# Loading the stacked queries and keys of an attention layer: six transfers from ScalarE's queue in place of nine from SyncE's

## The chip, the cores and the metric

The kernel runs on one core of one Trainium2 chip. The metric is device time in microseconds (us) of one execution. Lower is better. A core has five engines that run their own instruction streams and meet at semaphores: TensorE (PE in the rows, its weight loads are PEld), VectorE (DVE), ScalarE (ACT), GpSimd (POOL) and SyncE (SP), which here only issues transfers. Transfers run on 16 DMA engines that all queues share. A queue is written SPq, ACTq or POOLq after the engine that issues on it.

## The reference, cut to what matters

Two transformer blocks over x of shape (8, 512, 128), both with modulated layer norms. The first block has a linear attention and a mixture of 8 experts of which two are chosen for each token. The second block has the softmax attention that the change touches, and a mixture with one expert for each token:

```python
def _L1_attn_ref(x, Wq, bq, Wk, bk, Wv, bv, gamma, beta):
    H = 8
    B, S, D = x.shape            # 8, 512, 128
    dk = D // H                  # 16
    ...
    q = (xn @ Wq + bq).reshape(B, S, H, dk).transpose(0, 2, 1, 3)
    k = (xn @ Wk + bk).reshape(B, S, H, dk).transpose(0, 2, 1, 3)
    v = (xn @ Wv + bv).reshape(B, S, H, D).transpose(0, 2, 1, 3)
    scores = jnp.einsum('bhsd,bhtd->bhst', q, k) / jnp.sqrt(jnp.asarray(dk, x.dtype))
    p = jax.nn.softmax(scores, axis=-1)
    att = jnp.einsum('bhst,bhtd->bhsd', p, v)
    out = att.reshape(S, B, D, H).sum(axis=-1).reshape(B, S, D)
```

## The kernel before, in words

Each engine has an order written out by hand in the table ORDERS: a list of work items `kind.i.j` that its loop runs through. An engine never takes a later item before an earlier one, so an item that waits holds up everything behind it on its engine. The batches are taken in 4 pairs in the first block and one by one, 0 to 7, in the softmax attention.

For one batch i of that attention the items are these. `cpq` (TensorE, ScalarE, VectorE) makes q and k of all heads and splits each number into three bf16 terms, the last two of them made by `cpt` on GpSimd. `cto` (SP, line 554) writes the terms, 2 x 3 x 128 x 512 bf16, to the DRAM tensor `split`. `cst` (SP, lines 563 and 565) reads them back in another layout: for q and for k a stack of 96 partitions, six blocks of the 16 numbers of a head, where a partition holds 8 heads x 512 tokens = 8 KB. Every pair of blocks of the two stacks is one product of terms, so that one matmul with 96 rows gives the scores to nearly full precision. q's stack takes its three transfers of 48, 32 and 16 partitions (line 563), k's takes six of 16 partitions (line 565). `s1` (TensorE, line 1539) multiplies the stacks to the scores; `mx` (VectorE, line 1199) takes their maxima; `mt` (TensorE line 1545, ScalarE line 881, VectorE line 1217) puts the maxima into 12 more partitions of the stack; `s2` (TensorE, line 1555) makes the scores again, transposed and less their maxima; `ex` (ScalarE, line 888) takes the exponentials; `pv` (line 1565) multiplies them with v. Sixteen tiles of four `s2` and four `ex` make up a group of 4 heads.

There are two buffers for the stacks, so `cst` of batch i waits for the terms in DRAM (t_out) and, from batch 2 on, for the last `s2` that reads the buffer (c_s2x). `cto` of batch i + 1 waits until the stacks of batch i have landed (s_in), since both use the one tensor `split`. `s1` of a batch waits for s_in too.

Around it, the experts of the first block are still running on TensorE until about 425 us: `bw` (SP, line 520) loads the 514 KB of weights of one tile, `bh` and `by` (TensorE, lines 1504 and 1512) use them, with ScalarE's gelu (line 847) between the two. Five weight buffers go round, so `bw` waits for the `by` five tiles back. `bxl` (SP, line 529) loads sorted tokens, `byo` (SP, line 539) stores results, and GpSimd's indirect transfers (lines 691, 702) scatter and gather. Towards the end the routing of the last mixture does the same on lines 578 (`rxl`), 587 (`rw`), 590 (`ryo`) and 723 (`rsc`), with `rxt` (line 1404) and `rdx` (line 1410) on TensorE.

Of the kernel before, what the change touches and what calls it, by code (L numbers as in the profile page):

```python
# [12 lines left out]
B, S, D = 8, 512, 128  # L13
# [9 lines left out]
H1, DH1 = 8, 16  # L23
# [36 lines left out]
def same_rows(n):  # L60
# [198 lines left out]
def build(nc, io, out):  # L259
    ctx = ExitStack()  # L260
    with ctx:
# [101 lines left out]
        at = ab.o  # L363
# [8 lines left out]
        ex = ab.base[:, at:at + TILES * (E - 1)].rearrange("p (t e) -> p t e", t=TILES)  # L372
# [26 lines left out]
        qst = [stk[:, k] for k in range(2)]  # L399
        kst = [stk[:, 2 + k] for k in range(2)]  # L400
# [19 lines left out]
        split = dram("split", [2, 3, P, S], bf16)  # L420
# [24 lines left out]
        t_out = sem("c_terms_out")  # L445
        s_in = [sem(f"c_stacks_in{k}") for k in range(2)]
# [47 lines left out]
        def _(eng):  # L494
# [27 lines left out]
            for kind, i, j in ORDER["SP"]:  # L522
# [231 lines left out]
        def _(a):  # L754
# [5 lines left out]
            for kind, i, j in ORDER["ACT"]:  # L760
# [73 lines left out]
                if kind == "bxt":  # L834
                    q, n = TG * i + j, P * len(tiles_of(j))
# [5 lines left out]
                if kind == "bh":  # L841
                    n = TILES * i + j
# [33 lines left out]
                if kind == "mt":  # L876
                    b, h = group(i)
# [12 lines left out]
                if kind == "pvo":  # L890
# [3 lines left out]
                    b, h = group(i)  # L894
# [5 lines left out]
                if kind == "rxt":  # L900
                    n = P * len(tiles_of(j))
# [441 lines left out]
        def _(pe):  # L1343
# [3 lines left out]
            rows = identb[:, :].unsqueeze(1).broadcast_to([P, 4, P])  # L1347
# [18 lines left out]
            for kind, i, j in ORDER["PE"]:  # L1366
# [9 lines left out]
                if kind == "pc":  # L1376
                    pe.wait_ge(ld["mod"], 32)
                    pe.wait_ge(s_cs, 1)
                    for l in range(2):
                        for j6 in range(6):  # L1380
                            at = 8 * (6 * l + j6)
                            last = nc.tensor.matmul(ps[:, at:at + 8], wmod[:, l, D * j6:D * j6 + D], cs[:, l, :], start=True, stop=True)
                    last.then_inc(s_mod_c, 1)
                if kind in ("pm", "pr"):
                    n, rows2, js = (2 * i + j, (2 * j, 2 * j + 1), ROWS[i]) if kind == "pm" else (4, (0, 1), (3, 4))
                    pe.wait_ge(s_wide, n + 1)
                    for r in rows2:
                        for k in range(len(js)):
                            at = 512 * (r % 2) + D * k
# [263 lines left out]
```

## Time and profile before

| | |
|---|---|
| three runs, us | 791.36, 793.49, 792.43 |
| median | 792.43 |
| span of the profiled execution, first to last instruction | 674.4 us |
| TensorE busy | 601.6 us (89%) |
| VectorE busy | 481.1 us (71%) |
| ScalarE busy | 391.4 us (58%) |
| GpSimd busy | 330.5 us (49%) |
| mean granted TensorE clock | 0.978 |

The profile gives the span of its one execution and not that execution's own device time. The median less the span is 792.43 - 674.4 = 118.0 us; it lies before the first and after the last instruction that the span counts. All points in time below are microseconds from the span's start. A timeline row gives start, length, engine, line, operation, destination <- source and how many instructions are merged in it; square brackets give idle time of the engine before the row and what ended it.

### The profile page before, as it was taken

To read this page: it belongs to the slowest core of one execution; us is meant where nothing else is said; L and a number is where in the kernel's file an instruction comes from. 1 tells how busy PE (TensorE), PEld (TensorE's weight loads), DVE (VectorE), ACT (ScalarE), POOL (GpSimd) and SP (SyncE) were. 2 spreads that over 40 slices of the span, in tenths; PEclk is the share of its full clock that TensorE was granted. 3 is DMA by queue.
4 is the path that set the end of the run, shared out by engine and by line. 5 is a ranking of instruction groups with operands and counts; after the bars stand their busy time and mean duration, and the time that the engine had idled before them with its cause. 6 is when DMAs were issued, how large, how long until landed. Compare 5 with 4: busy or idle time off the path is not lost. (4 is left out here: it accounts for less than half of the span.)

```text
span 674.4 us, 11980 instructions
## 1 busy us (share of the span) xinstructions
PE 601.6 (89%) x3825; PEld 379.6 (56%) x3825; DVE 481.1 (71%) x1275; ACT 391.4 (58%) x866; POOL 330.5 (49%) x363
## 2 busy tenths in 40 slices
PE   8978988999999899798989899898999898889974
PEld 5656557988888797674345688332343324523332
DVE  4478876761794439388869734898998873889897
ACT  3444045889666575448778666676756576455510
POOL 5203378065478764704872601557456464064523
PEclk9999999999999999899999989999989998999999
DMA  8200415677789887949396868117411739311021
GB/s 336 116 1 2 141 44 168 213 247 251 249 304 311 283 315 238 285 151 252 119 232 196 167 234 268 40 40 173 70 25 36 170 114 214 102 47 48 17 63 31
DMA packets 47421, 106.40 MB, mean 158 GB/s; under 512 B 7440, under 2 KB 22608, under 8 KB 45824
## 3 DMA queue, kind: packets, MB, share of 16 engines
q1 hardware_dynamic: 41808, 94.82, 47.3%
q0 software_dynamic: 5120, 10.50, 4.9%
q8 instruction: 31, 0.51, 0.3%
q10 hardware_dynamic: 432, 0.34, 0.2%
q14 instruction: 30, 0.25, 0.1%
HBM read 80.26 MB, written 25.17 MB: 156 GB/s over the span
## 5 line engine op out<-in xcount | busy, mean ns | idle before, releaser
L1199 DVE TENSOR_REDUCE mxs<-PS 128x2 f32<-128x1024 f32 x128 | 151.8, 1220 | 46.3 <-PE PS L1539 46.0
L888 ACT ACTIVATE bufa<-PS 128x512 f32<-128x512 f32 x256 | 140.2, 602 | 60.7 <-PE PS L1555 52.7
L847 ACT ACTIVATE bufb<-PS,bufb 128x128 f32<-128x128 f32 x368 | 103.3, 379 | 65.1 <-PE PS L1504 64.5
L1504 PE MATMUL PS<-bufb 128*128 128x128 f32 x736 | 101.3, 286 | 12.4 <-DMA bufb<-in_experts_dram 10.7
L1504 PEld LDWEIGHTS PS<-bufb 128*128 128x128 f32 x736 | 93.0, 198 | 24.4 <-issue 14.2
L1512 PE MATMUL PS<-bufb 128*128 128x128 f32 x736 | 95.9, 278 | 2.2 <-ACT bufb L847 2.1
L1555 PE MATMUL PS<-stk 108*128 108x512 bf16 x256 | 85.2, 390 | 11.0 <-ACT bufa L888 8.4
L691 POOL DMA_INDIRECT slots_in<-bufb x64 | 65.7, 1026 | 55.2 <-DVE bufb L1145 37.0
L1512 PEld LDWEIGHTS PS<-bufb 128*128 128x128 f32 x736 | 89.4, 193 | 5.3 <-ACT bufb L847 3.9
L1539 PE MATMUL PS<-stk 96*128 96x512 bf16 x256 | 79.9, 399 | 11.2 <-DVE mxs L1199 7.3
L702 POOL DMA_INDIRECT bufb<-slots_out,bufb x64 | 61.9, 968 | 37.5 <-issue 26.7
L1565 PE MATMUL PS<-bufa,vv 128*32 128x512 f32 x512 | 69.1, 611 | 0.2 <-ACT bufa L895 0.2
L1555 PEld LDWEIGHTS PS<-stk 108*128 108x128 bf16 x256 | 23.1, 99 | 74.6 <-ACT bufa L888 44.8
L1539 PEld LDWEIGHTS PS<-stk 96*128 96x128 bf16 x256 | 21.0, 101 | 54.0 <-DVE mxs L1199 29.7
L657 POOL TENSOR_TENSOR rstd<-rstd,mhalf 128x8 f32<-128x8 f32 x12 | 20.7, 1726 | 58.6 <-DVE rstd L973 58.6
L1352 PE MATMUL PS<-identb 128*128 128x512 bf16 x187 | 45.9, 391 | 2.2 <-POOL dm L615 2.2
L1608 PE MATMUL PS<-bufb 128*128 128x512 f32 x64 | 30.6, 605 | 2.9 <-DVE bufb L1311 2.5
L1352 PEld LDWEIGHTS PS<-identb 128*128 128x128 bf16 x187 | 18.7, 101 | 21.8 <-issue 3.1
L839 ACT ACTIVATE bufb<-PS,cols 128x512 f32<-128x512 f32 (+1 forms) x24 | 18.6, 776 | 18.0 <-PE PS L1497 17.7
L731 POOL DMA_INDIRECT bufb<-slots_out,bufb x16 | 16.2, 1013 | 25.1 <-DMA slots_out<-bufb 20.9
L1565 PEld LDWEIGHTS PS<-bufa,vv 128*32 128x32 f32 x512 | 10.6, 108 | 23.2 <-issue 20.6
L737 POOL CAST terms<-rest 128x1024 bf16<-128x1024 f32 x8 | 8.3, 1042 | 30.2 <-DVE rest L1185 30.2
(292 smaller groups left out, 958.2 us busy)
## 6 DMA issues: line engine op xcount, KB each, us to landing
bufb<-in_experts_dram SPq DMA_DIRECT2D x92, 514.0 KB, 5.1
slots_out<-bufb SPq DMA_DIRECT2D x30, 256.0 KB, 2.9
stk<-split SPq DMA_DIRECT2D x56, 128.0 KB, 8.4
bufb<-slots_in SPq DMA_DIRECT2D x25, 256.0 KB, 4.5
split<-terms SPq DMA_DIRECT2D x8, 768.0 KB, 4.0
slots_in<-hb SPq DMA_DIRECT2D x2, 1536.0 KB, 9.5
stk<-split SPq DMA_DIRECT2D x8, 384.0 KB, 6.9
X<-in_x_dram SPq DMA_DIRECT2D x4, 512.0 KB, 6.5
```

Of the source, the lines that this page charges most:

```text
L691: nc.gpsimd.indirect_dma_start(xs[i % 2], bass.IndirectOffsetOnAxis(ap=posi[i][:, k, t:t + 1], axis=0), z2[:, t, :], None).then_inc(sc_out ...
L702: nc.gpsimd.indirect_dma_start(yt[:, k, t, :], None, yd[i % 2], bass.IndirectOffsetOnAxis(ap=posi[i][:, k, t:t + 1], axis=0)).then_inc(ga_ ...
L847: last = nc.scalar.activation(hs[:, n % HR, fc, :], ps[:, P * fc:P * fc + P], ACT.Gelu_apprx_tanh, bias=ws[:, n % WR, F + fc:F + fc + 1])
L888: nc.scalar.activation(probs[:, i % PR, j, :], psum("s2", i, j), ACT.Exp, scale=DH1 ** -0.5)\
L1199: nc.vector.tensor_reduce(mxs[:, gr % 2, 2 * j:2 * j + 2, h], psum("s1", i, j).rearrange("p (c n) -> p c n", c=2), axis=AX.X, op=ALU.max)\
L1352: nc.tensor.matmul(place, identb[:, :], rows, start=True, stop=True)
L1504: last = nc.tensor.matmul(ps[:, P * fc:P * fc + P], ws[:, n % WR, P * fc:P * fc + P], xq[:, q % 2, P * x:P * x + P], start=True, stop=True)
L1512: last = nc.tensor.matmul(y, hs[:, n % HR, fc, :], ws[:, n % WR, W2AT + D * fc:W2AT + D * fc + D], start=(fc == 0), stop=(fc == FC - 1))
L1539: last = nc.tensor.matmul(ps[:, S * (c % 2):S * (c % 2) + S], qst[b % 2][0:KS, h, P * c:P * c + P], kst[b % 2][0:KS, h, :], start=True, st ...
L1555: nc.tensor.matmul(ps, kst[b % 2][0:KM, h, P * c:P * c + P], qst[b % 2][0:KM, h, :], start=True, stop=True).then_inc(c_s2x, 1)
L1565: last = nc.tensor.matmul(bank(7)[32 * hh:32 * hh + 32, :], vv[:, b % 3, j, 4 * k + hh, :], probs[:, n % PR, hh, :], start=(j == 0), stop= ...
L1608: last = nc.tensor.matmul(ps[:, 512 * e2:512 * e2 + 512], xTd[i % 2][:, P * j:P * j + P], expT[:, 4 * e2:4 * e2 + 4, :].rearrange("p e d - ...
```

## The change

The item `cst` leaves SP's order and enters ScalarE's, at eight new places. Its waits stay the same. It issues six transfers in place of nine: the 96 partitions are now blocks of 48, 16 and 32, laid at partitions 32 to 79, 80 to 95 and 0 to 31, and each block is filled by one transfer for q and one for k. The transfer for k of the first block reads one term's 16 rows three times, that of the third block another term's 16 rows twice. This is written as a source with a leading dimension of 3 or 2 that does not move. What is multiplied stays the same; only the order of the blocks in the 96 rows differs. The semaphore s_in is counted to 96 in place of 144. Bytes are the same: 96 partitions x 8 KB x 2 for each batch.

```diff
 "ACT": ...
-        cpq.0.0 bh.2.8 bh.2.9 by.2.1 bxt.2.3 bh.2.10 bgt.3.0 bh.2.11 bh.2.12 bxt.2.4 bh.2.13 by.2.2 cpq.1.0 bh.2.14 bh.2.15
+        cpq.0.0 bh.2.8 bh.2.9 by.2.1 bxt.2.3 bh.2.10 bgt.3.0 bh.2.11 bh.2.12 bxt.2.4 cst.0.0 bh.2.13 by.2.2 cpq.1.0 bh.2.14 bh.2.15
...
 "SP": ...
-        bw.2.13 bw.2.14 bw.2.15 bxl.2.5 cst.0.0 bw.2.16 bw.2.17 bw.2.18 bw.2.19 bw.2.20 byo.2.1 cto.1.0 byo.2.2 byo.2.3 bw.2.21
+        bw.2.13 bw.2.14 bw.2.15 bxl.2.5 bw.2.16 bw.2.17 bw.2.18 bw.2.19 bw.2.20 byo.2.1 cto.1.0 byo.2.2 byo.2.3 bw.2.21
...
 in SP's loop:
-                        eng.wait_ge(s_in[(i - 1) % 2], 144 * ((i - 1) // 2 + 1))
+                        eng.wait_ge(s_in[(i - 1) % 2], 96 * ((i - 1) // 2 + 1))
                     eng.dma_start(split.rearrange("t j p n -> p t j n"), terms[:, :, :, :]).then_inc(t_out, 16)
-                if kind == "cst":
-                    eng.wait_ge(t_out, 16 * (i + 1))
-                    if i >= 2:
-                        eng.wait_ge(c_s2x, 32 * (i - 1))
-
-                    def rows(t, j0, j1):
-                        return split[t, j0:j1].rearrange("j (i h) n -> (j i) h n", h=H1)
-                    for lo, js in ((0, 3), (3, 2), (5, 1)):
-                        eng.dma_start(qst[i % 2][DH1 * lo:DH1 * (lo + js), :, :], rows(0, 0, js)).then_inc(s_in[i % 2], 16)
-                    for at, k in enumerate((0, 0, 0, 1, 1, 2)):
-                        eng.dma_start(kst[i % 2][DH1 * at:DH1 * at + DH1, :, :], rows(1, k, k + 1))\
-                            .then_inc(s_in[i % 2], 16)
 in ScalarE's loop:
+                if kind == "cst":
+                    a.wait_ge(t_out, 16 * (i + 1))
+                    if i >= 2:
+                        a.wait_ge(c_s2x, 32 * (i - 1))
+
+                    def rows(t, j0, j1):
+                        return split[t, j0:j1].rearrange("j (i h) n -> (j i) h n", h=H1)
+                    for lo, js, k in ((2, 3, 0), (5, 1, 2), (0, 2, 1)):
+                        at = slice(DH1 * lo, DH1 * (lo + js))
+                        nc.scalar.dma_start(qst[i % 2][at, :, :], rows(0, 0, js)).then_inc(s_in[i % 2], 16)
+                        same = rows(1, k, k + 1).unsqueeze(0).broadcast_to([js, DH1, H1, S])
+                        nc.scalar.dma_start(kst[i % 2][at, :, :], same).then_inc(s_in[i % 2], 16)
 in TensorE's loop (s1):
-                        pe.wait_ge(s_in[b % 2], 144 * (b // 2 + 1))
+                        pe.wait_ge(s_in[b % 2], 96 * (b // 2 + 1))
```

On ScalarE, at batch 0 (line 839 prepares the sorted tokens of a group, line 847 is the gelu, 813 and 815 are the new transfers of q and k):

```order
 L847 ACTIVATE bufb<-PS,bufb 128x128 x8
 L839 ACTIVATE bufb<-PS,cols 128x512
+L813 DMA stk<-split 48x4096
+L815 DMA stk<-split 48x1x4096
+L813 DMA stk<-split 16x4096
+L815 DMA stk<-split 16x4096
+L813 DMA stk<-split 32x4096
+L815 DMA stk<-split 32x1x4096
 L847 ACTIVATE bufb<-PS,bufb 128x128 x4
 L855 COPY bufb<-PS 128x512
```

The six transfers stand between two items of the experts, ahead of a gelu. On ScalarE at batch 5, before (line 888 takes exponentials, 881 copies the maxima into the stack, 895 copies finished values, 866 prepares the next pair):

```order
L895 COPY bufa<-PS 128x8x64
L888 ACTIVATE bufa<-PS 128x512 x12
L881 COPY stk<-PS 12x512
L895 COPY bufa<-PS 128x8x64
L888 ACTIVATE bufa<-PS 128x512 x6
L866 ACTIVATE xTa<-PS,cols 128x2x256 x2
```

and the same place now:

```order
L895 COPY bufa<-PS 128x8x64
L888 ACTIVATE bufa<-PS 128x512 x11
L813 DMA stk<-split 48x4096
L815 DMA stk<-split 48x1x4096
L813 DMA stk<-split 16x4096
L815 DMA stk<-split 16x4096
L813 DMA stk<-split 32x4096
L815 DMA stk<-split 32x1x4096
L888 ACTIVATE bufa<-PS 128x512
L881 COPY stk<-PS 12x512
L895 COPY bufa<-PS 128x8x64
L888 ACTIVATE bufa<-PS 128x512 x6
```

The six stand ahead of the last exponential of the second group of batch 3, and so ahead of the copy of the maxima behind it. Batches 3, 6 and 7 have the same form. On SP at batch 0 (line 520 loads weights, each with a register load and three more instructions ahead of it, 529 loads sorted tokens):

```order
 L520 DMA bufb<-in_experts_dram 128x1028
 L529 DMA bufb<-slots_in 128x384
-L563 DMA stk<-split 48x4096
-L563 DMA stk<-split 32x4096
-L563 DMA stk<-split 16x4096
-L565 DMA stk<-split 16x4096 x6
 L519 TENSOR_LOAD bufb
 L519 ISA x2
```

Nine transfers and their waits are gone from between the sorted tokens and the next weights.

## Rows read from the trace of the kernel before

**Rows 1.** The page's first line.

```profile
span 674.4 us, 11980 instructions
```

**Rows 2.** Timeline of TensorE: its waits, and s1 of batches 0, 1, 4 to 6.

```profile
283.61 2.05 PE L1504 MATMUL PS<-bufb 128*128 128x128 f32 x8 [4.64 <-DMA bufb<-in_experts_dram]
285.45 1.91 PE L1539 MATMUL PS<-stk 96*128 96x512 bf16 x4
...
318.36 0.60 PE L1539 MATMUL PS<-stk 96*128 96x512 bf16 x2
...
388.21 1.85 PE L1504 MATMUL PS<-bufb 128*128 128x128 f32 x8 [2.90 <-DMA bufb<-in_experts_dram]
...
468.84 0.59 PE L1539 MATMUL PS<-stk 96*128 96x512 bf16 x2 [1.53 <-DMA stk<-split]
...
498.12 0.61 PE L1539 MATMUL PS<-stk 96*128 96x512 bf16 x2 [0.33 <-ACT bufb L915]
...
538.51 0.60 PE L1539 MATMUL PS<-stk 96*128 96x512 bf16 x2
...
569.66 1.09 PE L1404 MATMUL PS<-identf,bufb 128*128 128x128 f32 x4 [2.16 <-DMA bufb<-slots_in]
```

**Rows 3.** The chain that ended last, 455 to 560: start, us, what.

```profile
459.50 9.21 DMA stk<-split
...
482.92 0.59 ACT stk L881
...
552.86 3.83 DMA split<-terms
```

**Rows 4.** Timeline of SP's queue: start, us, issue.

```profile
267.25 1.43 SPq L563 DMA_DIRECT2D stk<-split  x3
...
523.82 1.23 SPq L563 DMA_DIRECT2D stk<-split  x3
```

**Rows 5.** Timeline of ScalarE's queue: an issue at the start of the kernel.

```profile
4.13 0.34 ACTq L759 DMA_DIRECT2D bufa<-in_L_attn_b_proj_dram  x1
```

**Rows 6.** Windows: stretch, engines' busy us, clock, share of 16 DMA engines, GB/s.

```profile
14.00:16.00 2.00, 1.77 (x18) 1.53 (x15) 0.00 (x0) 1.08 (x2) 0.00 (x0) 1.00 1.00 418
...
483.00:491.50 8.50, 7.65 (x53) 4.01 (x46) 8.10 (x28) 6.60 (x12) 0.59 (x1) 1.00 1.05 169
```

**Rows 7.** Packets, and issues: queue, count, KB each, us to landing.

```profile
DMA packets 47421, 106.40 MB, mean 158 GB/s; under 512 B 7440, under 2 KB 22608, under 8 KB 45824
...
bufb<-in_experts_dram SPq DMA_DIRECT2D x92, 514.0 KB, 5.1
...
stk<-rest SPq DMA_DIRECT2D x4, 48.0 KB
...
bufb<-in_L_ffn_b_dram SPq DMA_DIRECT2D x8, 4.0 KB
...
stk<-in_c_dram ACTq DMA_DIRECT2D x1, 8.0 KB, 3.3
cols<-in_cols_dram SPq DMA_DIRECT2D x1, 11.0 KB, 5.3
```

**Rows 8.** Instructions of line 520, the weights: from issue to landing.

```profile
DMA to landing us min/median/max: 3.2/5.1/8.8
```

**Rows 9.** Timeline of ScalarE at five of the eight places.

```profile
269.57 0.78 ACT L839 ACTIVATE bufb<-PS,cols 128x512 f32<-128x512 f32 x1 [2.25 <-PE PS L1497]
...
303.99 1.28 ACT L888 ACT_TABLE_LOAD   x1 [1.23 <-PE PS L1555]
...
451.77 4.27 ACT L888 ACTIVATE bufa<-PS 128x512 f32<-128x512 f32 x8 [0.77 <-PE PS L1565]
...
481.62 0.60 ACT L888 ACTIVATE bufa<-PS 128x512 f32<-128x512 f32 x1 [0.55 <-PE PS L1555]
...
552.87 3.14 ACT L888 ACTIVATE bufa<-PS 128x512 f32<-128x512 f32 x6 [0.72 <-PE PS L1555]
```

**Rows 10.** Timeline of VectorE behind batch 2.

```profile
348.26 0.61 DVE L1151 SCALAR_TENSOR_TENSOR bufb<-bufb,hb 128x128 f32<-128x128 f32 x2 [3.06 <-DMA bufb<-slots_out,bufb]
```

More of the change, by code:

```diff
@@ L142 @@
         bxt.2.1 bh.1.22 bh.2.0 by.1.5 bh.2.1 bh.2.2 bh.2.3 ctr.0.0 btr.3.0 bh.2.4 bh.2.5 by.2.0 bh.2.6 blg.3.0 bh.2.7 bxt.2.2
-        cpq.0.0 bh.2.8 bh.2.9 by.2.1 bxt.2.3 bh.2.10 bgt.3.0 bh.2.11 bh.2.12 bxt.2.4 bh.2.13 by.2.2 cpq.1.0 bh.2.14 bh.2.15
-        bxt.2.5 bh.2.16 bh.2.17 bh.2.18 by.2.3 bh.2.19 bh.2.20 ctr.1.0 mt.0.0 by.2.4 ex.0.0 ex.0.1 ex.0.2 bh.2.21 bh.2.22 ex.0.3
+        cpq.0.0 bh.2.8 bh.2.9 by.2.1 bxt.2.3 bh.2.10 bgt.3.0 bh.2.11 bh.2.12 bxt.2.4 cst.0.0 bh.2.13 by.2.2 cpq.1.0 bh.2.14 bh.2.15
+        bxt.2.5 bh.2.16 bh.2.17 bh.2.18 by.2.3 bh.2.19 bh.2.20 ctr.1.0 mt.0.0 cst.1.0 by.2.4 ex.0.0 ex.0.1 ex.0.2 bh.2.21 bh.2.22 ex.0.3
         ex.1.0 ex.1.1 ex.1.2 by.2.5 ex.1.3 ex.2.0 ex.2.1 ex.2.2 ex.2.3 ex.3.0 mt.1.0 ex.3.1 ex.3.2 ex.3.3 cpq.2.0 ex.4.0 ex.4.1
-        ex.4.2 ex.4.3 pvo.0.0 ex.5.0 ex.5.1 ex.5.2 ex.5.3 ex.6.0 ex.6.1 ex.6.2 ex.6.3 ex.7.0 mt.2.0 ex.7.1 ex.7.2 ex.7.3 ex.8.0
+        ex.4.2 ex.4.3 pvo.0.0 ex.5.0 ex.5.1 ex.5.2 ex.5.3 ex.6.0 ex.6.1 ex.6.2 ex.6.3 ex.7.0 mt.2.0 ex.7.1 ex.7.2 ex.7.3 ex.8.0 cst.2.0
         ex.8.1 ex.8.2 pvo.1.0 ex.8.3 cpq.3.0 ex.9.0 ex.9.1 ex.9.2 ex.9.3 ex.10.0 ex.10.1 ex.10.2 bxt.3.0 bh.3.0 bh.3.1 bh.3.2
         bh.3.3 ex.10.3 mt.3.0 ex.11.0 by.3.0 bxt.3.1 ex.11.1 ex.11.2 bxt.3.2 ex.11.3 ex.12.0 ex.12.1 ex.12.2 ex.12.3 pvo.2.0
-        ex.13.0 ex.13.1 ex.13.2 ex.13.3 ex.14.0 ex.14.1 ex.14.2 ex.14.3 ex.15.0 ex.15.1 ex.15.2 ex.15.3 bh.3.4 bh.3.5 bh.3.6
+        ex.13.0 ex.13.1 ex.13.2 ex.13.3 ex.14.0 ex.14.1 ex.14.2 ex.14.3 ex.15.0 ex.15.1 ex.15.2 cst.3.0 ex.15.3 bh.3.4 bh.3.5 bh.3.6
         bh.3.7 bh.3.8 bxt.3.3 by.3.1 bh.3.9 bh.3.10 mt.4.0 bh.3.11 ctr.2.0 bh.3.12 bh.3.13 by.3.2 bh.3.14 bh.3.15 cpq.4.0
@@ L153 @@
         ex.19.2 ex.19.3 ex.20.0 ex.20.1 ex.20.2 ex.20.3 ex.21.0 mt.7.0 ex.21.1 ex.21.2 pvo.4.0 ex.21.3 ex.22.0 ex.22.1 ex.22.2
-        ex.22.3 ex.23.0 ex.23.1 ex.23.2 ex.23.3 ex.24.0 ex.24.1 pvo.5.0 ex.24.2 ex.24.3 ex.25.0 ex.25.1 ex.25.2 ex.25.3 ex.26.0
+        ex.22.3 ex.23.0 ex.23.1 ex.23.2 ex.23.3 cst.4.0 ex.24.0 ex.24.1 pvo.5.0 ex.24.2 ex.24.3 ex.25.0 ex.25.1 ex.25.2 ex.25.3 ex.26.0
         ex.26.1 ex.26.2 ex.26.3 ex.27.0 ex.27.1 ex.27.2 ex.27.3 ex.28.0 ex.28.1 ex.28.2 ex.28.3 pvo.6.0 ex.29.0 ex.29.1 ex.29.2
-        ex.29.3 ex.30.0 ex.30.1 ex.30.2 ex.30.3 ex.31.0 ex.31.1 ex.31.2 ex.31.3 mt.8.0 pvo.7.0 ex.32.0 ex.32.1 ex.32.2 ex.32.3
+        ex.29.3 ex.30.0 ex.30.1 ex.30.2 ex.30.3 ex.31.0 ex.31.1 ex.31.2 cst.5.0 ex.31.3 mt.8.0 pvo.7.0 ex.32.0 ex.32.1 ex.32.2 ex.32.3
         ex.33.0 ex.33.1 ctr.3.0 ex.33.2 ex.33.3 ex.34.0 ex.34.1 ex.34.2 ex.34.3 dtr.0.0 ex.35.0 ex.35.1 ex.35.2 mt.9.0 ex.35.3
         ex.36.0 ex.36.1 ex.36.2 ex.36.3 ex.37.0 pvo.8.0 ex.37.1 ex.37.2 ex.37.3 cpq.6.0 ex.38.0 ex.38.1 ex.38.2 ex.38.3 dtr.1.0
-        ex.39.0 mt.10.0 ex.39.1 ex.39.2 ex.39.3 ex.40.0 ex.40.1 ex.40.2 pvo.9.0 ex.40.3 ex.41.0 ex.41.1 ex.41.2 ex.41.3 ex.42.0
+        ex.39.0 mt.10.0 ex.39.1 ex.39.2 cst.6.0 ex.39.3 ex.40.0 ex.40.1 ex.40.2 pvo.9.0 ex.40.3 ex.41.0 ex.41.1 ex.41.2 ex.41.3 ex.42.0
         ex.42.1 ex.42.2 ex.42.3 ex.43.0 mt.11.0 ex.43.1 ex.43.2 ex.43.3 cpq.7.0 ex.44.0 pvo.10.0 ex.44.1 ex.44.2 ex.44.3 ex.45.0
-        ex.45.1 ex.45.2 ex.45.3 ex.46.0 ex.46.1 ex.46.2 ex.46.3 ex.47.0 ex.47.1 ex.47.2 ex.47.3 mt.12.0 pvo.11.0 ex.48.0 ex.48.1
+        ex.45.1 ex.45.2 ex.45.3 ex.46.0 ex.46.1 ex.46.2 ex.46.3 ex.47.0 ex.47.1 ex.47.2 cst.7.0 ex.47.3 mt.12.0 pvo.11.0 ex.48.0 ex.48.1
         ex.48.2 ex.48.3 rxt.0.0 ex.49.0 ex.49.1 rxt.0.1 rdx.0.0 ex.49.2 ex.49.3 rdx.0.1 ex.50.0 ex.50.1 ex.50.2 rxt.0.2 rxt.0.3
@@ L206 @@
         bw.2.3 byo.1.4 byo.1.5 bw.2.4 bxl.2.3 bw.2.5 bxl.2.4 bw.2.6 bw.2.7 bw.2.8 byo.2.0 bw.2.9 bw.2.10 bw.2.11 bw.2.12 cto.0.0
-        bw.2.13 bw.2.14 bw.2.15 bxl.2.5 cst.0.0 bw.2.16 bw.2.17 bw.2.18 bw.2.19 bw.2.20 byo.2.1 cto.1.0 byo.2.2 byo.2.3 bw.2.21
-        bw.2.22 byo.2.4 cst.1.0 bw.3.0 bw.3.1 byo.2.5 bw.3.2 bw.3.3 cto.2.0 bxl.3.0 bw.3.4 bxl.3.1 cst.2.0 bxl.3.2 bxl.3.3
-        bw.3.5 bxl.3.4 bw.3.6 cto.3.0 bw.3.7 bw.3.8 cst.3.0 bw.3.9 bw.3.10 bw.3.11 bw.3.12 byo.3.0 bw.3.13 bw.3.14 bw.3.15
+        bw.2.13 bw.2.14 bw.2.15 bxl.2.5 bw.2.16 bw.2.17 bw.2.18 bw.2.19 bw.2.20 byo.2.1 cto.1.0 byo.2.2 byo.2.3 bw.2.21
+        bw.2.22 byo.2.4 bw.3.0 bw.3.1 byo.2.5 bw.3.2 bw.3.3 cto.2.0 bxl.3.0 bw.3.4 bxl.3.1 bxl.3.2 bxl.3.3
+        bw.3.5 bxl.3.4 bw.3.6 cto.3.0 bw.3.7 bw.3.8 bw.3.9 bw.3.10 bw.3.11 bw.3.12 byo.3.0 bw.3.13 bw.3.14 bw.3.15
         byo.3.1 bw.3.16 bxl.3.5 byo.3.2 bw.3.17 bw.3.18 bw.3.19 bw.3.20 cto.4.0 bw.3.21 bw.3.22 byo.3.3 byo.3.4 byo.3.5 dl.0.0
-        cst.4.0 cto.5.0 cst.5.0 cto.6.0 cst.6.0 dws.0.0 rw.0.0 rw.0.1 cto.7.0 rxl.0.0 rxl.0.1 cst.7.0 rxl.0.2 rxl.0.3 rw.0.2
+        cto.5.0 cto.6.0 dws.0.0 rw.0.0 rw.0.1 cto.7.0 rxl.0.0 rxl.0.1 rxl.0.2 rxl.0.3 rw.0.2
         ryo.0.0 ryo.0.1 rxl.0.4 rw.0.3 rxl.0.5 ryo.0.2 rw.0.4 rw.0.5 ryo.0.3 ryo.0.4 ryo.0.5 rst.0.0 dst.2.0 rst.1.0 dst.3.0
```

## The prediction

> **What bounds the kernel now.** I read the page first: TensorE is busy for 601.6 of 674.4 us [rows 1], so the kernel is bound by TensorE wherever TensorE doesn't wait, and elsewhere by the chain that makes it wait. Next I listed TensorE's timeline at its waits, to see which of them the change can touch [rows 2]. A bracket there is idle time and what ended it. Two stand at weights of the experts (4.64 us at 283.61, 2.90 at 388.21), one at the stacks of batch 4 (1.53 at 468.84), one at sorted tokens that SP issues right behind the stacks of batch 7 (2.16 at 569.66). Together 4.64 + 2.90 + 1.53 + 2.16 = 11.2 us: all that better transfers could give back. The s1 of batches 0, 1, 5 and 6 start with no wait for the stacks. Then I read the chain of waits towards the end [rows 3]. It runs through the stack's last transfer of batch 4 (459.50 + 9.21 = 468.71), ScalarE's copy of the maxima at 482.92 and the last write of split, which ends at 552.86 + 3.83 = 556.69. What makes ScalarE late there, or stretches a landing, is paid in full.
>
> **SP: nine issues less per batch.** Three issues take 1.43 us, 0.48 each [rows 4], so SP is about 4.3 us freer at each of eight places. TensorE's rows wait for landings, not for SP's issues, and `bw` waits for a buffer in any case. I cost this at nothing of its own; where it could give something, at the weights of 283.61, TensorE's wait is followed by s1 of batch 0 at 285.45, and so hidden behind the stacks reckoned next.
>
> **The transfers: on how many engines?** This decides the case. The trace has no transfer that repeats its source, so I look at what it has with few rows. The page counts 7,440 packets under 512 B [rows 7]. If each transfer closes with one small packet on each of 16 engines, the 454 issues of the page's list (291 on SP's queue, 160 on GpSimd's, 3 on ScalarE's, added up) make 7,264; small rows of the loads of cols (128) and of c (128) make it 7,520. 80 are missing. The eight loads of L_ffn_b with 8 rows and the four of stk<-rest with 12 rows [rows 7] give just that if they run on 8 and on 12 engines: 8 x 8 + 4 x 4 = 80. So a transfer here can run on fewer engines than 16, as many as its outer count. The new k transfers have an outer count of 3 and 2 on the source side. I take it that they run on 3 and 2 engines; their 16 rows of 8 KB then fall on each of these.
>
> The Trainium skill says the same ("DMA: Bandwidth & Descriptors", "Why a DMA increments its semaphore by 16 and not by 1"): the number of engines is the largest up to 16 that divides the outer counts of both sides. Its "Rules for kernel authors" names a leading broadcast of c copies as one that confines a transfer to c engines. The count of 80 agrees for plain rows; for a broadcast no run here shows it yet.
>
> Packets on the busiest engine, per batch: q of 48, 16 and 32 rows gives 3 + 1 + 2, k of 16 rows 1, the two broadcasts 16 + 16: 39. Before, each engine had 192 / 16 = 12.
>
> What a packet of 8 KB costs there is bounded by two windows [rows 6]. In 14 to 16 the 16 engines, always busy, move 418 GB/s: 26.1 each, 8,192 B in 0.314 us. In 483 to 491.5, with the stacks nearly alone, they are as busy (1.05) at 169 GB/s: 0.814 us. I read the low rate as crowding, since 16 engines then write to 16 neighbouring partitions. I choose 0.814 for the seven plain packets that all engines take, and 0.314 for the 32 that two engines take while the others rest: 7 x 0.814 + 32 x 0.314 = 15.7 us. Ahead and behind comes the fixed part: the quickest weights land in 3.2 us [rows 8], less 8 packets of 4,112 B at 26.1 GB/s (1.26), is 1.9. So a stack takes 17.6 us from its first issue. Bounds: all 39 at 0.314, 14.1; all at 0.814, 33.7. The kernel before, by the same reckoning: 12 x 0.814 + 1.9 = 11.7.
>
> **ScalarE: six issues more per batch.** One there takes 0.34 us [rows 5], SP's 0.48. I take 0.45, so 2.7 us per batch in an engine that runs in order.
>
> **Batch by batch**, in the times of before:
> - 0: ScalarE comes to it at 269.57 + 0.78 = 270.35 [rows 9]; SP began at 267.25 [rows 4]. Landing 270.4 + 17.6 = 288.0. The five weights that follow on SP add 5 x 8 packets x 0.157 = 6.3 to the same engines if nothing overlaps: 294.3. Middle 291.1 against 285.45: +5.7 (2.5 to 8.8). The wait of 4.64 is then still there under another name.
> - 1: behind the exponentials, before the table load at 303.99, so at 303.99 - 1.23 = 302.8. Lands 320.4 against 318.36: +2.0. The 2.7 of ScalarE less 1.23 of idle lies inside it.
> - 2: between exponentials. VectorE waits 3.06 us for gathers just behind [rows 10], which hides most of the 2.7: +0.5 (bounds 0 and 2.7).
> - 3: the place is some 50 us ahead of the s1 that needs it, among experts that wait for weights (2.90): 0. The broadcasts share two engines with these weights, which may lengthen the wait, and SP's freer queue may shorten it: -2.9 to +3.
> - 4: behind the eight exponentials that end at 451.77 + 4.27 = 456.0 [rows 9]; lands 473.6 against 468.84: +4.8.
> - 5: ahead of the exponential of 481.62, and so of the copy of the maxima at 482.92, which is on the chain. 2.7 less the idle 0.55: +2.1. The stack, from 481.1, lands at 498.7, before the s1 that now stands at 498.12 + 2.1.
> - 6: SP issued at 523.82 [rows 4], and ScalarE's place is within a microsecond of that. Lands 541.4 against 538.51: 2.9 late on TensorE. The chain runs through GpSimd's scatters to 552.86, not through this s1, and the next item is later than this one by more: 0 (up to 2.9).
> - 7: the six issues stand among the exponentials from 552.87 on [rows 9] and wait for split until 556.69, so ScalarE stops for about 2 us and issues for 2.7. The stack lands at 556.7 + 17.6 = 574.3. The s1 of batch 7 follows the row of 569.66 by 0.9, at 570.5: +3.8. The 2.16 us of before lies inside it, for the sorted tokens no longer stand behind the stack in a queue.
>
> Sum: 5.7 + 2.0 + 0.5 + 0 + 4.8 + 2.1 + 0 + 3.8 = +18.9 us. It is made against an execution with a span of 674.4; what lies around the span, 792.43 - 674.4 = 118.0, the change doesn't touch. So 792.4 + 18.9 = **811 us**. With all packets at 0.314 the same list gives 2.2 + 1.0 + 0.5 + 0 + 1.3 + 2.1 + 0 + 0.3 = 7.4: 800.
>
> **Rivals.**
> - *The broadcasts run on all 16 engines and the waits go.* A transfer of 48 destination rows could be cut by its destination. Then the six are as quick as the nine, weights and tokens stand behind fewer issues, and up to 11.2 us come back; against it ScalarE costs 0.5 + 2.1 and about 1 at batches 1 and 7 each. -11.2 + 4.6: 786; 781 if nothing is paid on ScalarE. For it speaks that every wait of the 11.2 stands at a transfer from SP's queue; against it the count of 80. This is the faster end. Chance 0.16.
> - *16 engines, but a draw.* ScalarE's 2.7 us at each place take back what the waits give: 790 to 795. Chance 0.11.
> - *The crowding stays.* If 8 KB cost 0.814 us for a lone engine too, because the slow rate is that of one engine reading this tensor, a stack takes 33.7 us. Then s1 is late by 25 (batch 0: 310.4), 18 (1), about 13 (2), 21 (4: 489.7), 17 (5: 514.8), 19 (6: 557.5) and 20 (7: 590.4): +133, 925. Halfway, at 0.5 us a packet, a stack takes 21.4: 9.5 + 5.8 + 0.5 + 8.6 + 4.4 + 3 + 7.6 = +39, 832. For it: no row shows an engine alone. Against: the same engines move other 8 KB worth of rows at 26 GB/s. Chance 0.18 for everything above 830.
>
> **How the numbers follow.** My own case, 2 and 3 engines with quick packets, has 0.55, with a range of 797 to 830. 0.16 lies around 781 to 789, 0.11 around 790 to 795, 0.18 above 830. To leave out no more than 2 in 10, the range reaches from 787 to 850: about 0.1 stays below, 0.08 above. No change is within 0.3%, or 2.4 us, about what a measurement here can tell: 790.0 to 794.8. Faster 0.17, same 0.10, slower 0.73.
>
> **What would show it.** In the profile after: packets under 512 B fall by more than three transfers per batch (8 x 3 x 16 = 384) by 13 + 14 for each batch's two broadcasts (216), since these close on 3 and 2 engines; if only 384 go, all 16 engines are at work and I am wrong. The issues of stk<-split on ScalarE's queue land after some 14 to 18 us. TensorE has waits for stk<-split at batches 0, 1, 4 and 7, of 2 to 8 us. The DMA share between 491 and 499 is low, about 2 of 16 engines. ScalarE shows 2.7 us of idle at each place, and the copy of the maxima of 482.92 is later by 2. If the wait at 283.61 is gone with s1 at once behind it, the case is the first rival.

## The result and the profile after

| | before | changed |
|---|---|---|
| five runs each, median, us | 791.36 (787.52 to 793.49) | 827.09 (823.54 to 836.72) |
| ratio, 95% interval | 1 | 1.0514 (1.0463 to 1.0566) |
| second profile: execution, span, us | 780.70, 779.0 | 816.74, 815.0 |

Slower by 5.1% by the ratio, about 41 us; the medians of the table lie 35.7 us apart, and the spans of the two second profiles 36.0. 18.9 was forecast: the sign was right, the size about half of what came. The first profile of the changed kernel is of an execution of 836.7 us, longer than the other four; its span is read nowhere below, and a second profile stands in its place.

The first profile of the kernel before had a span of 674.4 us [rows 1] against timed runs of 787.5 to 793.5, so it has a second one too. Its first line and its line of busy times:

```profile
span 779.0 us, 11980 instructions
PE 632.0 (81%) x3825; PEld 394.6 (51%) x3825; DVE 475.3 (61%) x1275; ACT 392.5 (50%) x866; POOL 331.3 (43%) x363
```

The same lines of the changed kernel's second page:

```profile
span 815.0 us, 11956 instructions
PE 640.1 (79%) x3825; PEld 395.7 (49%) x3825; DVE 473.7 (58%) x1275; ACT 392.3 (48%) x866; POOL 330.1 (41%) x363
...
DMA packets 46820, 106.39 MB, mean 131 GB/s; under 512 B 6840, under 2 KB 22008, under 8 KB 45224
```

Of the 36.0 us between these two, TensorE is busy for 8.1 more (640.1 - 632.0, the same matmuls at a lower clock) and idle for 27.9 more. The packets under 512 B are 6,840: 7,440 less 384 for three transfers per batch less 216, as worked out for sources that run on 3 and 2 engines. The transfers themselves show it at batch 5, whose stack has the engines nearly to itself; windows of the changed kernel, with TensorE's busy time (instructions), its clock, the share of the 16 DMA engines and GB/s:

```profile
606.50:610.50 4.00, 3.92 (x15) 0.56 0.19 74
612.00:616.00 4.00, 3.86 (x24) 1.00 0.13 53
```

A share of 0.19 is 3 engines and one of 0.13 is 2. They move 74 / 3 = 24.7 and 53 / 2 = 26.5 GB/s each, so a packet of 8,192 B takes 0.33 and 0.31 us there. The kernel before, in the middle of the same batch's stack:

```profile
580.00:585.00 5.00, 4.72 (x32) 1.00 1.04 144
```

All 16 engines are busy, at 144 / 16 = 9.0 GB/s each, 0.91 us per packet.

What TensorE waited for, in the changed kernel (in total, times, longest):

```profile
PE PS L1539 <- DMA stk<-split: 24.1, 4, 14.0
```

and in the kernel before:

```profile
PE PS L1504 <- DMA bufb<-in_experts_dram: 9.5, 5, 4.8
...
PE PS L1539 <- DMA stk<-split: 1.7, 1, 1.7
```

The four waits in TensorE's timeline of the changed kernel, at s1 of batches 0, 1, 4 and 7. The first three answer to the rows of 285.45, 318.36 and 468.84 in [rows 2], and s1 of batch 7 stands right behind the row of 569.66 there:

```profile
350.79 1.87 PE L1539 MATMUL PS<-stk 96*128 96x512 bf16 x4 [13.99 <-DMA stk<-split]
...
388.75 1.01 PE L1539 MATMUL PS<-stk 96*128 96x512 bf16 x2 [4.09 <-DMA stk<-split]
...
584.71 1.01 PE L1539 MATMUL PS<-stk 96*128 96x512 bf16 x2 [5.18 <-DMA stk<-split]
...
713.89 0.59 PE L1539 MATMUL PS<-stk 96*128 96x512 bf16 x2 [0.86 <-DMA stk<-split]
```

Two matmuls of s1 take 0.6 at a clock of 1.00 [rows 2]. Behind the waits of 4.09 and 5.18 they take 1.01; in the 1.8 to 2.3 us behind each of the first three waits the granted clock is 0.50, the lower of its two levels. ScalarE's timeline of the changed kernel at batch 6, which answers to [rows 9]:

```profile
645.40 1.08 ACT L888 ACTIVATE bufa<-PS 128x512 f32<-128x512 f32 x2
646.75 0.31 ACTq L813 DMA_DIRECT2D stk<-split  x1
647.09 0.73 ACTq L815 DMA_DIRECT2D stk<-split  x1
647.85 0.45 ACTq L813 DMA_DIRECT2D stk<-split  x1
648.33 0.45 ACTq L815 DMA_DIRECT2D stk<-split  x1
648.80 0.44 ACTq L813 DMA_DIRECT2D stk<-split  x1
649.28 0.64 ACTq L815 DMA_DIRECT2D stk<-split  x1
649.97 0.60 ACT L888 ACTIVATE bufa<-PS 128x512 f32<-128x512 f32 x1 [3.48 <-issue]
```

The six issues leave ScalarE idle for 3.48 us ahead of its next exponential. At the eight places of this profile the idle time is 2.7 to 3.8 us.

How long a stack takes, from the start of its first issue to the last landing that its semaphore counts, us, for batches 0 to 7 (for the kernel before and the changed one from the second profiles; a dash where the last records are missing). At batches 2 and 6, and partly at batch 1, some landings are not on record, and the last one that is counts:

| | 0 | 1 | 2 | 3 | 4 | 5 | 6 | 7 |
|---|---|---|---|---|---|---|---|---|
| before | 14.3 | 12.3 | 12.7 | 12.1 | 13.7 | 12.1 | 12.4 | 12.5 |
| changed | 27.4 | 22.3 | 19.2 | 19.6 | 19.0 | 17.0 | - | 18.5 |
| interleaved, ScalarE (act_rows) | 12.9 | 10.4 | 10.4 | 9.9 | 11.7 | 9.8 | 9.7 | 9.8 |
| interleaved, SP (sp_rows) | 13.1 | 10.2 | 12.4 | 9.9 | 11.2 | 10.2 | 9.4 | 10.1 |

### The profile page after: what moved, and what is told of

The parts are those of the page before. It is cut to its first block and busy times, and to the rows that moved or that the text cites. A ratio compares the mean times of both kernels' runs of the same rounds, so it can differ in the third digit from the quotient of the medians.

```text
span 834.9 us, 11956 instructions
## 1 busy us (share of the span) xinstructions
PE 651.7 (78%) x3825; PEld 404.3 (48%) x3825; DVE 471.5 (56%) x1275; ACT 392.1 (47%) x866; POOL 327.6 (39%) x363
## 2 busy tenths in 40 slices
DMA packets 46820, 106.39 MB, mean 127 GB/s; under 512 B 6840, under 2 KB 22008, under 8 KB 45224
## 5 line engine op out<-in xcount | busy, mean ns | idle before, releaser
L1504 PE MATMUL PS<-bufb 128*128 128x128 f32 x736 | 106.8, 296 | 35.6 <-ACT bufb L847 10.5
L1555 PE MATMUL PS<-stk 108*128 108x512 bf16 x256 | 93.0, 421 | 51.7 <-ACT bufa L888 32.2
L1504 PEld LDWEIGHTS PS<-bufb 128*128 128x128 f32 x736 | 98.6, 208 | 47.7 <-issue 22.0
L1512 PE MATMUL PS<-bufb 128*128 128x128 f32 x736 | 102.1, 288 | 20.7 <-ACT bufb L847 10.2
L1539 PE MATMUL PS<-stk 96*128 96x512 bf16 x256 | 87.5, 432 | 29.8 <-DMA stk<-split 12.9
L1512 PEld LDWEIGHTS PS<-bufb 128*128 128x128 f32 x736 | 94.9, 202 | 24.8 <-ACT bufb L847 12.1
L1555 PEld LDWEIGHTS PS<-stk 108*128 108x128 bf16 x256 | 23.9, 103 | 127.8 <-ACT bufa L888 65.7
L690 POOL DMA_INDIRECT bufb<-slots_out,bufb x64 | 61.0, 953 | 61.8 <-issue 35.9
L1565 PE MATMUL PS<-bufa,vv 128*32 128x512 f32 x512 | 80.0, 699 | 6.0 <-ACT bufa L888 5.8
L1539 PEld LDWEIGHTS PS<-stk 96*128 96x128 bf16 x256 | 22.4, 105 | 76.8 <-issue 42.7
L645 POOL TENSOR_TENSOR rstd<-rstd,mhalf 128x8 f32<-128x8 f32 x12 | 20.7, 1725 | 62.6 <-DVE rstd L973 62.5
L647 POOL TENSOR_TENSOR mom<-st 128x16 f32<-128x16 f32 x11 | 2.4, 217 | 76.4 <-DVE st L957 76.4
L839 ACT ACTIVATE bufb<-PS,cols 128x512 f32<-128x512 f32 (+1 forms) x24 | 18.6, 774 | 26.0 <-PE PS L1497 19.2
L1565 PEld LDWEIGHTS PS<-bufa,vv 128*32 128x32 f32 x512 | 11.2, 114 | 32.7 <-issue 29.9
```

The source lines that it names most:

```text
L690: nc.gpsimd.indirect_dma_start(yt[:, k, t, :], None, yd[i % 2], bass.IndirectOffsetOnAxis(ap=posi[i][:, k, t:t + 1], axis=0)).then_inc(ga_ ...
L1504: last = nc.tensor.matmul(ps[:, P * fc:P * fc + P], ws[:, n % WR, P * fc:P * fc + P], xq[:, q % 2, P * x:P * x + P], start=True, stop=True)
L1512: last = nc.tensor.matmul(y, hs[:, n % HR, fc, :], ws[:, n % WR, W2AT + D * fc:W2AT + D * fc + D], start=(fc == 0), stop=(fc == FC - 1))
L1555: nc.tensor.matmul(ps, kst[b % 2][0:KM, h, P * c:P * c + P], qst[b % 2][0:KM, h, :], start=True, stop=True).then_inc(c_s2x, 1)
L1565: last = nc.tensor.matmul(bank(7)[32 * hh:32 * hh + 32, :], vv[:, b % 3, j, 4 * k + hh, :], probs[:, n % PR, hh, :], start=(j == 0), stop= ...
```

## The experiments

**before_again**: the kernel before, no edit.

> The kernel before, unchanged, for a second profile of it. Its three timed runs are 118 us longer than the span that its profile shows (792.4 against 674.4), while the changed kernel's execution of 836.7 has a span of 834.9. Theory P: the 118 us lie around the span; then the span is again about 674 and ScalarE has no long idle with no cause shown. Theory Q: the 118 us are stalls inside an ordinary execution, and the profile shown before was of an execution without them; then the span is 786 to 792, and engines stand idle for reasons the profile can't name already ahead of the first stack.

780.70 us, span 779.0: theory Q, though below its 786 to 792, as the timed runs beside it were (779.5 to 786.2). ScalarE's timeline at two places where it stands idle ahead of the first stack:

```profile
166.27 1.14 ACT L847 ACTIVATE bufb<-PS,bufb 128x128 f32<-128x128 f32 x4 [12.38 <-remote]
...
299.99 1.14 ACT L847 ACTIVATE bufb<-PS,bufb 128x128 f32<-128x128 f32 x4 [11.16 <-remote]
```

"remote" is a release whose origin the profile can't name. ScalarE has 20 such waits, 95.0 us in all, and the first profile has none. So the 118.0 us of the prediction were not time around the span: an execution's time and its span differ by 1.7 us (780.70 - 779.0). From here on all comparisons are with this profile.

**sp_bcast**, **act_plain** and **act_rows** take the change apart. sp_bcast leaves `cst` on SP at its old places, in the new form (here and below the cuts leave out waits and semaphores):

```diff
-for lo, js in ((0, 3), (3, 2), (5, 1)):   # nine transfers
+for lo, js, k in ((2, 3, 0), (5, 1, 2), (0, 2, 1)):
+    at = slice(DH1 * lo, DH1 * (lo + js))
+    eng.dma_start(qst[i % 2][at, :, :], rows(0, 0, js))
+    eng.dma_start(kst[i % 2][at, :, :], rows(1, k, k + 1).unsqueeze(0).broadcast_to([js, DH1, H1, S]))
```

> The new six transfers with their repeated sources, but issued by SP at the old places. Theory 1 (the repeated sources run on 3 and 2 engines, and the stacks land late): still slower, 1.03 to 1.05, 815 to 832 us, with TensorE waiting for stk<-split. Theory 2 (the issues on ScalarE cost the time): no slower than before, 0.99 to 1.005. Packets under 512 B 6840 in either.

act_plain is the changed kernel without repeated sources:

```diff
-same = rows(1, k, k + 1).unsqueeze(0).broadcast_to([js, DH1, H1, S])
-nc.scalar.dma_start(kst[i % 2][at, :, :], same)
+for j in range(lo, lo + js):
+    nc.scalar.dma_start(kst[i % 2][DH1 * j:DH1 * j + DH1, :, :], rows(1, k, k + 1))
```

> The new blocks on ScalarE's queue at the new places, but each repeated block of k filled by transfers of 16 rows without repetition, so nine transfers per batch. Theory 1 (few engines): back to 0.99 to 1.01, 783 to 799 us. Theory 2 (ScalarE's issues): nine in place of six, so 1.05 to 1.08, 830 to 850 us.

act_rows keeps six transfers on ScalarE and puts the row outermost:

```diff
-nc.scalar.dma_start(qst[i % 2][at, :, :], rows(0, 0, js))
-same = rows(1, k, k + 1).unsqueeze(0).broadcast_to([js, DH1, H1, S])
+mixed = split[0, 0:js].rearrange("j (i h) n -> i j h n", h=H1)
+nc.scalar.dma_start(qst[i % 2][at, :, :], mixed)
+same = rows(1, k, k + 1).unsqueeze(1).broadcast_to([DH1, js, H1, S])
```

> Six transfers on ScalarE's queue at the new places, with the rows of a block interleaved (row outermost, term inside), so that the repeated source has 16 as its outer count. What is multiplied is the same. Theory 1: the broadcasts run on 16 engines, packets under 512 B are 7440 - 384 = 7056, stacks land within 14 us of the issue, and the time is that of before or under it, 0.98 to 1.005. Theory 2: as slow as the changed kernel, 1.04 to 1.06.

Measured: sp_bcast 1.0391 (1.0339 to 1.0443), act_plain 1.0216 (1.0154 to 1.0279), act_rows 1.0170 (1.0109 to 1.0231). Neither theory alone: few engines cost most of it, and what is left without them on ScalarE's queue is 1.7 to 2.2%, which theory 1 had at nothing. The two parts add up: 1.0391 x 1.0170 = 1.057, the changed kernel had 1.051. Packets under 512 B of act_rows are 7,056, as expected, and its stacks land in 9.7 to 12.9 us (table). They then wait for TensorE, not TensorE for them:

```profile
PE PS L1498 <- DMA bufb<-slots_in: 1.4, 1, 1.4
PE PS L1540 <- DMA stk<-split: 1.4, 1, 1.4
PE PS L1505 <- DMA bufb<-in_experts_dram: 1.4, 3, 0.7
```

In sp_bcast the loss shows at other instructions than in the changed kernel, for the weights stand in the same queue behind the slow packets:

```profile
PE PS L1504 <- DMA bufb<-in_experts_dram: 26.4, 4, 13.2
...
PE PS L1539 <- DMA stk<-split: 14.7, 3, 7.5
```

**after_again**: the changed kernel, no edit.

> The changed kernel, unchanged, for a second profile, since its first shows a stall at 101 us, far ahead of the first stack. Both theories: span 820 to 828, the stacks land 17 to 21 us after their first issue (batch 0 some 24 to 27), and first issue at about 322 us in place of 330.

816.74 us, span 815.0, a little under the range; first issue at 323.3. The landings are in the table: 17.0 to 22.3, batch 0 27.4.

**sp_rows** is act_rows on SP at the old places, and **sp_mixed** interleaves the block of 48 alone (shown against sp_bcast, in short):

```diff
 for lo, js, k in ((2, 3, 0), (5, 1, 2), (0, 2, 1)):
     of_q, same = rows(0, 0, js), rows(1, k, k + 1).unsqueeze(0).broadcast_to([js, DH1, H1, S])
+    if js == 3:
+        of_q = split[0, 0:js].rearrange("j (i h) n -> i j h n", h=H1)
+        same = rows(1, k, k + 1).unsqueeze(1).broadcast_to([DH1, js, H1, S])
```

> The six transfers with the rows of a block interleaved, so on 16 engines, issued by SP at the old places. Theory 1a (with 16 engines the six land some 10 us after the first issue in place of 12.5, and all that the interleaved kernel lost on ScalarE's queue, 1.7%, was ScalarE's issuing): 0.985 to 0.998. Theory 1b (the queue is what counts: on SP's queue the stacks stand among weights as before, and 1.7% is due to where the issues moved to on the DMA side): 0.998 to 1.01, landing as late as before.

> By SP at the old places: only the block of 48 is interleaved (16 engines), the block of 32 keeps its leading repetition (2 engines). The busiest engine has 3 + 3 + 1 + 1 + 2 + 16 = 26 packets of 8 KB: by the sum of the prediction 10 x 0.814 + 16 x 0.314 + 1.9 = 15.1 us to land, some 2.5 us later than before. Theory 1 (the time follows the lateness of the busiest engine): between the two others on SP's queue, 1.005 to 1.02. A rival by which any repeated leading dimension costs the same (a slow path in the issue or the engine): as slow as with both, 1.03 to 1.045.

sp_rows: 0.9963 (0.9927 to 0.9999), landing in 9.4 to 13.1 us: theory 1a, and the only form of the stacks here whose interval lies below 1, if by a hair. It differs from sp_bcast, on the same queue at the same places, in the order of rows alone, and that is worth 4.3%. sp_mixed: 1.0177 (1.0108 to 1.0246), between the two others on SP's queue, as theory 1 had it and not as slow as with both. A fixed price for each transfer with a leading repetition would give a time between them too; the landings speak for the busiest engine. Its stacks land in 20.3 us at batch 0 and in 12.9 to 17.3 at the others, batch 6 aside, whose last landings are not on record; 15.1 was worked out.

**act_dummy**: the kernel before, and at the eight places of ScalarE's order six small transfers that nothing uses.

```diff
+if kind == "dum":
+    for n, rows in enumerate((48, 48, 16, 16, 32, 32)):
+        a.dma_start(dummy[i, n, 0:rows], io["experts"][0, 0:rows, 0:64]).then_inc(c_dummy, 16)
```

> The kernel before, stacks and all by SP, plus six small transfers at each of the eight new places in ScalarE's order: DRAM to DRAM, 48, 48, 16, 16, 32 and 32 rows of 256 B, of data that nothing uses, with no waits. It leaves on ScalarE the time of the issues alone. Theory A (ScalarE's issuing, 2.6 us or more at each place, is what costs the 1.7%): 1.012 to 1.025. Theory B (the waits for the terms and for the free buffer, now in ScalarE's order, cost it): 1.000 to 1.008.

1.0189 (1.0121 to 1.0257): theory A. Issuing alone costs what act_rows lost, with stacks untouched on SP's queue. ScalarE's timeline ahead of batch 7:

```profile
672.19 2.65 ACT L893 ACTIVATE bufa<-PS 128x512 f32<-128x512 f32 x5 [0.72 <-PE PS L1561]
674.25 3.74 ACTq L820 DMA_DIRECT2D dummy_rows<-in_experts_dram  x6
678.04 0.60 ACT L893 ACTIVATE bufa<-PS 128x512 f32<-128x512 f32 x1 [3.19 <-issue]
```

TensorE's at the same place:

```profile
674.36 1.07 PE L1571 MATMUL PS<-bufa,vv 128*32 128x512 f32 x8
675.26 0.39 PE L1551 MATMUL PS<-identb,mxt 128*12 128x128 bf16 x4
678.88 1.71 PE L1571 MATMUL PS<-bufa,vv 128*32 128x512 f32 x8 [3.24 <-ACT bufa L893]
```

and three windows of it (columns as in [rows 6]):

```profile
674.50:679.20 4.70, 1.46 (x16) 0.48 (x14) 0.39 (x3) 1.48 (x3) 0.00 (x0) 1.00 0.83 182
679.20:682.60 3.40, 3.40 (x15) 1.33 (x8) 0.70 (x3) 1.99 (x5) 0.00 (x0) 0.50 1.08 192
682.60:692.00 9.40, 9.31 (x70) 6.04 (x69) 3.36 (x15) 7.09 (x14) 4.74 (x2) 1.00 0.44 107
```

ScalarE's 3.2 us become 3.24 on TensorE, which is then busy all of the next 3.4 us at a clock of 0.50, the lower of its two levels: eight matmuls that took 1.07 take 1.71. That second price stands under no wait. Span and mean clock of the kernel before, and of this one:

```profile
core 0: 779.0 us, clock 0.908
```

```profile
core 0: 798.3 us, clock 0.885
```

Time at half clock is (1 - 0.908) x 2 x 779.0 = 143 us before, (1 - 0.885) x 2 x 798.3 = 184 here; 41 us more of it are worth up to 20 us of matmuls by this estimate, and TensorE is busy for 649.4 us in place of 632.0. Its idle time grew by 1.9 us only, since other waits are shorter here (at the weights, 4.8 us in place of 9.5). The timed runs say the same: the mean clock is 0.894 over four of act_dummy and 0.911 over the 17 of the kernel before beside them.

**dummy_spread**, **dummy_three** and **rows_spread** ask whether it is the sum of ScalarE's time or the pause. The first puts one of the six behind each of the next items, the second issues three:

```diff
-dum.7.0 ex.47.3 mt.12.0 pvo.11.0 ex.48.0 ex.48.1 ex.48.2 ex.48.3
+dum.7.0 ex.47.3 dum.7.1 mt.12.0 pvo.11.0 ex.48.0 dum.7.2 ex.48.1 dum.7.3 ex.48.2 dum.7.4 ex.48.3 dum.7.5
```

```diff
-for n, rows in enumerate((48, 48, 16, 16, 32, 32)):
+for n, rows in enumerate((48, 16, 32)):
```

> As the kernel with six small unused transfers at each place of ScalarE's order, but the six are spread: one behind each of the next five exponentials or gelus. ScalarE's time for issues is the same 3.7 us per batch. Theory S (the sum of ScalarE's time counts): again 1.015 to 1.022. Theory C (a pause of 3.7 us in a row is what stops TensorE, which then runs at half clock for a while; pauses of 0.6 us fall into ScalarE's idle gaps): 1.000 to 1.008, and less half clock than the 186 us of the six in a row.

> The same with three small transfers at each place in place of six, in a row, about 1.8 us of ScalarE each time. Theory S (in proportion): 1.008 to 1.011. Theory C (short pauses are hidden or nearly so): 1.000 to 1.006.

rows_spread does the same to act_rows:

```diff
-cst.7.0 ex.47.3 mt.12.0 pvo.11.0 ex.48.0 ex.48.1 ex.48.2 ex.48.3
+cst.7.0 ex.47.3 cst.7.1 mt.12.0 pvo.11.0 ex.48.0 cst.7.2 ex.48.1 cst.7.3 ex.48.2 cst.7.4 ex.48.3 cst.7.5
```

> The interleaved six transfers on ScalarE's queue, spread over the next exponentials for batches 2, 4, 5, 6 and 7 (in a row for 0, 1 and 3, where gelus of the experts follow). The six in a row cost 1.7% in all. Theory S: 1.012 to 1.02 again. Theory C: 1.002 to 1.010, since five of eight pauses are gone and the stacks of the interleaved form have 6 to 20 us to spare.

Measured: dummy_spread 0.9957 (0.9909 to 1.0004), dummy_three 1.0008 (0.9964 to 1.0051), rows_spread 1.0042 (0.9997 to 1.0087). Theory S fails on all three, and theory C's ranges hold but for dummy_spread, which came out a little under. They were timed beside 25 runs of the kernel before with a median of 789.89, act_dummy beside runs with one of 780.34; six in a row was not timed again beside them. dummy_spread also rules out that the traffic of the unused transfers costs the time in act_dummy, for it moves the same. ScalarE's timeline of dummy_spread at the same place:

```profile
666.39 0.60 ACT L896 ACTIVATE bufa<-PS 128x512 f32<-128x512 f32 x1
666.41 0.58 ACTq L823 DMA_DIRECT2D dummy_rows<-in_experts_dram  x1
667.25 0.58 ACT L889 COPY stk<-PS 12x512 bf16<-12x512 bf16 x1 [0.26 <-PE PS L1554]
```

The issue starts 0.02 us behind the start of the exponential ahead of it and runs beside it for as long as that lasts. So one issue behind one exponential costs ScalarE next to nothing; the second and later ones of a row stop it. Spreading therefore takes away most of ScalarE's stopped time along with the long pause, and dummy_spread doesn't tell the two apart. dummy_three nearly does: its rows stop ScalarE for 1.2 to 2.3 us, against 3.2 to 3.7 for six in act_dummy, and by the sum of that time it should still lose some 0.8%, above its interval.

## Why the prediction was wrong

The sign and the path of the late stacks were right, but two terms of the sum were too small, by about as much each. The late stacks stood at 16.3 us and cost some 27. ScalarE's six issues stood at 2.6, since most of them were taken for hidden, and cost 13 to 15. What stands behind a stop of TensorE, matmuls at the lower clock, had no term. Batch by batch, s1 of batches 0, 1, 4, 5, 6 and 7 starts 12.3, 16.5, 23.8, 29.4, 37.8 and 36.4 us later in the second profile of the changed kernel than in that of the kernel before; the sum had 5.7, 7.7, 13.0, 15.1, 15.1 and 18.9 by then. These are single executions, and the 17 timed runs of the kernel before in one group spread over 11 us, but the largest misses are batch 0 and the stretch from batch 4 to 6.

- *On how many engines*: right. The count that told it (80 packets) foretold 6,840. The rule of the Trainium skill ("DMA: Bandwidth & Descriptors", "Why a DMA increments its semaphore by 16 and not by 1") agrees with this trace for repeated sources as well, and sp_mixed's 6,944 (7,440 - 384 - 8 x 14) is one more case.
- *How long a stack takes*: right. 17.6 us was worked out, 17.0 to 22.3 measured behind batch 0. The two prices of a packet held at batch 5: 0.31 to 0.33 for 0.314 where 2 or 3 engines work alone, 0.91 for 0.814 where all 16 do. The rival of 0.5 us per packet came out at 832, nearest to the time, but with 21.4 us per stack it is not what happened.
- *Late stacks*: the path was right, the size was not. For terms of 5.7 + 2.0 + 4.8 + 3.8 = 16.3, TensorE's waits show 14.0, 4.1, 5.2 and 0.9, 24.1 in all and 22.4 more than before. Batch 0 is the miss: I took the middle between weights that cost the stack nothing and weights that cost it all, 20.7 us to land, and measured 27.4, more than with all (23.9). From 332 to 340, with stack and weights on the engines together, all 16 are busy and move 252 GB/s, 15.8 each, where the 6.3 us for the weights were worked out at 26.1; that this makes the difference was not tried. By the ratios, 1.0514 / 1.0170, the few engines cost 3.4%, some 27 us. The 4 or 5 us beyond the waits I put down to TensorE's clock: that it is 0.50 behind three of them is shown, what this costs is argued.
- *ScalarE's six issues*: this step failed. It had 2.7 us per batch, of which 2.1 and 0.5 stood in the sum, since I looked for them on the chain of waits and took the rest for hidden. A row of six takes 3.2 to 3.7 us, and alone costs 1.7 to 1.9%, 13 to 15 us. In act_dummy it stops TensorE itself at batches 3, 4, 5 and 7, for 2.62, 2.12, 2.03 and 3.24 us, of which the sum had that of batch 5 alone: the matmuls there follow on the exponentials that the row holds up. And within 1.4 us of the end of each stop the granted clock falls to 0.50 and matmuls run at it, for which the sum has no term at all.
- *Issues from another engine*: the Trainium skill ("DMA: Bandwidth & Descriptors", "Issuing engines are not separate DMA queues") says that this saves the time of initiating, "which is usually small relative to the DMA itself". Small it was, 3.2 to 3.7 us per batch against 17 to 27 to land; on the engine that took it over it cost 1.9% in a row and nothing spread out.
- *The base*: wrong. An ordinary execution has the 118.0 us, or most of them, inside its span. The sum did not hang on it much: the s1 of batches 0, 1, 4, 5 and 7 have 3.8, 3.6, 0.1, 4.3 and 1.0 us from landing to start in the second profile, much as in the first.

The first rival (16 engines, waits gone) didn't happen for this kernel, but sp_rows builds it: its weights' waits fell from 9.5 to 4.5 us, and of the 11.2 us hoped for there, 0.4%, some 3 us, came.

## What to carry to other kernels

In a transfer that repeats its source, put the rows outermost and the repetition inside; the multiplication doesn't care in which order rows stand, as long as both operands have the same. Issues on a computing engine cost nothing measurable here one at a time, each behind an instruction that runs as long as the issue, nor three in a row; six in a row stopped that engine and what it feeds, and TensorE paid once more in its clock. Before a sum is made on a profile, hold its span against the timed runs: where they lie far apart, find out first what fills the gap.

## What the runs showed of the hardware that was not expected

In the second profiles of both kernels, releases that other engines wait for come late while GpSimd runs a row of indirect transfers: all 20 waits of ScalarE in the kernel before whose origin the profile can't name, 95.0 us, run beside such transfers, and so do 16 of 18, 94.1 of 94.5 us, in the changed kernel. In the kernel before, TensorE's two matmuls of s1 are recorded at 412.10:

```profile
412.10 1.06 PE L1539 MATMUL PS<-stk 96*128 96x512 bf16 x2
422.71 1.46 PE L1555 MATMUL PS<-stk 108*128 108x512 bf16 x3 [9.55 <-ACT bufa L888]
```

VectorE, which only waits for these two, starts here:

```profile
421.65 1.23 DVE L1199 TENSOR_REDUCE mxs<-PS 128x2 f32<-128x1024 f32 x1 [12.87 <-remote]
```

and GpSimd's last gather of the row stands at

```profile
417.43 0.95 POOL L702 DMA_INDIRECT bufb<-slots_out,bufb  x1 [0.30 <-issue]
```

ScalarE resumes within 0.1 us of VectorE, at 421.57, some 3.2 us behind that gather's end. The first profile has as many gathers and none of these stalls. That this costs the 105 us between the two (779.0 - 674.4), and why, was not tried and stays open.

The interleaved repeated sources land quicker than the plain nine: 9.8 to 10.4 us at batches 1, 3, 5 and 7 on ScalarE's queue, where act_plain has 10.9 to 12.1, for the same bytes over the same engines. The last of six issues ends about 0.5 us sooner than the last of nine; what makes the rest was not tried either.
